# Table rows made in the stage of the keys, and attention weights put into the sums' masks

## The chip, the cores and the metric

The kernel runs on one core of one Trainium2 chip. The metric is the device time of one execution in microseconds (us). Of an engine, PE is TensorE's matmuls, PEld its weight loads, DVE is VectorE, ACT is ScalarE, POOL is GpSimd, and SP is the engine that only issues DMAs and waits.

## The reference

A stack of four graph layers over 3125 nodes with 64 features and 100000 edges, sorted by destination; each layer is followed by a residual and a layer norm. Only the first matters here, an attention layer over 8 relations:

```python
h = x @ Wr                                  # per relation r, of 8
s = h @ a_src
d = h @ a_dst
e = jax.nn.leaky_relu(s[src] + d[dst], negative_slope=0.2)
e = jnp.where(mask, e, -jnp.inf)            # mask: edges of relation r, and self loops
m = jax.ops.segment_max(e, dst, num_segments=N)
w = jnp.where(mask, jnp.exp(e - m[dst]), 0.0)
denom = jax.ops.segment_sum(w, dst, num_segments=N)
out = out + jax.ops.segment_sum((w / denom[dst])[:, None] * h[src], dst, num_segments=N) + br
```

## The kernel before, in words

Every stage is a block of five instruction streams, one per engine, written out by hand, with semaphores between them. A stage begins when all five engines have left the one before it. The order of an engine's instructions is the order of the code.

The head of the program, one stage after the other:

- `constants`: iota rows and identities.
- `edge_keys` (L142): SP loads destination, source and type of all edges. DVE makes from them a record of 7 words for each edge (`rec`, written to `meta` in DRAM) and two one-hot arrays, and PE multiplies these (98 matmuls into `hist`, L277) to count the edges of each of 196 groups of 16 nodes. The counts go to `count_row` in DRAM.
- `schedule` (L291): the counts come back to all partitions (`cnt`, L320). DVE makes from them, in some 130 small steps, the table of visits: a visit is 128 consecutive edges of one group. SP writes it (L323 to L327).
- `group_records`: it does work only if the edges are unsorted, which these are not.
- `node_tables` (L393): SP loads weights and nodes (L432). For each of 25 tiles of 128 nodes, PE makes h of all 8 relations (`h_ps`, L466) and both scores (`s_ps`, L467), ACT and DVE copy them out of PSUM into `rows` (8 relations, each 64 features, a one, and the source score: 66 words) and `score`, and SP writes the rows to `table` in DRAM. `rows` has two buffers. Then the scores go to DRAM (L445) and come back in another layout (`tab`, L449), and PE sorts them by visit with one-hot masks (`visit_hot`, L509; matmuls at L474).

Then `attention` (L702), 122 batches of 8 visits. The streams run skewed: in step n of the loop, an engine works for batches n-2 to n+4. POOL gathers the 128 table rows of each visit (`hs`, L830, six buffers, with 8 gathers in a batch). DVE makes, for all 8 visits at once, `miss` (is the edge's key not this column), and `far`, which is -2^100 at a miss and the source score at a hit (L1036). PE transposes `far` into `masked`; DVE takes its maximum (`top`, L1029); ACT turns it into a 0/1 mask in the other orientation (`hit_t`, L850), with which PE picks the maxima per edge (`picked`). From these DVE makes the exponent `lz` of each edge's weight (L1066). Beside this, for each visit PE counts neighbours (`near`, L971) into one PSUM tile that goes on from visit to visit, and ACT copies it out (`keep`, L868) before the next may be added: the matmul of visit i+1 waits for the copy of visit i, and the copy waits for the matmul. ACT also makes the 0/1 mask for the sums (`hit`, L860, two instructions of 4 visits), the weights (`weight`, L882) and the fading factors (`fade`, L891). DVE multiplies the gathered rows by the weights (`hw`, L1122), PE multiplies `hit` by `hw` (`sums`, L943), and DVE adds the result to `acc` (L1017). After each batch ACT writes eight counts to `slots` in DRAM (L873).

The other three layers follow and are not touched.

## Time and profile before

| | us |
|---|---|
| median of 3 runs (lowest, highest) | 4082.32 (4075.14, 4087.51) |
| the profiled execution | 4076.66 |
| its span | 4074.7 |
| busy in the span: PE, PEld | 2867.3, 2008.6 |
| busy in the span: DVE, ACT, POOL | 2338.2, 1459.4, 2325.4 |
| first matmul of `hist` | 44.49 |
| end of DVE's visits table | 100.07 |
| first and last row copy from `h_ps` on ACT | 126.79, 177.99 |
| last update of `acc` on DVE | 1900.2 |

The span is the time from the first to the last instruction of one execution; 1.96 us lie around it. The shares of busy time are an average over stages with different limits: the head is a chain of stages in which one engine works and the others wait, and in the attention all five work at once.

### The profile page before, as it was taken

To read this page: it belongs to the slowest core of one execution; us is meant where nothing else is said; L and a number is where in the kernel's file an instruction comes from. 1 tells how busy PE (TensorE), PEld (TensorE's weight loads), DVE (VectorE), ACT (ScalarE), POOL (GpSimd) and SP (SyncE) were. 2 spreads that over 40 slices of the span, in tenths; PEclk is the share of its full clock that TensorE was granted. 3 is DMA by queue.
4 is the path that set the end of the run, shared out by engine and by line. 5 is a ranking of instruction groups with operands and counts; after the bars stand their busy time and mean duration, and the time that the engine had idled before them with its cause. 6 is when DMAs were issued, how large, how long until landed. Compare 5 with 4: busy or idle time off the path is not lost. (4 is left out here: it accounts for less than half of the span.)

```text
span 4074.7 us, 77799 instructions
## 1 busy us (share of the span) xinstructions
PE 2867.3 (70%) x16134; PEld 2008.6 (49%) x16135; DVE 2338.2 (57%) x8613; ACT 1459.4 (36%) x3275; POOL 2325.4 (57%) x1835
## 2 busy tenths in 40 slices
PE   1627677777767677656779959887878787777752
PEld 1315455555555555444334436666666566666631
DVE  7138888888888888776342244444444444444423
ACT  0115555454455455443000004333333333333320
POOL 0046676666666666550000006888888888888880
PEclk9955555555555565556879978888888989898976
DMA  1354334333433333784614304555555555555543
GB/s 45 101 111 118 96 105 116 105 105 107 115 102 105 110 105 105 84 103 110 206 49 124 98 13 51 53 54 53 54 54 54 54 53 54 53 54 54 54 41 77
DMA packets 651838, 336.52 MB, mean 83 GB/s; under 512 B 436752, under 2 KB 612163, under 8 KB 650820
## 3 DMA queue, kind: packets, MB, share of 16 engines
q0 software_dynamic: 148736, 86.57, 22.1%
q1 hardware_dynamic: 453094, 119.03, 13.8%
q10 hardware_dynamic: 49824, 129.15, 8.3%
q14 instruction: 152, 1.25, 0.1%
q8 instruction: 32, 0.52, 0.1%
HBM read 156.42 MB, written 202.84 MB: 88 GB/s over the span
## 5 line engine op out<-in xcount | busy, mean ns | idle before, releaser
L2129 POOL DMA_INDIRECT sums<-el_rows,el_idx x816 | 1269.1, 1555 | 648.0 <-DVE el_rows L2343 399.3
L830 POOL DMA_INDIRECT at_hs<-table,at_rec_s x976 | 1048.7, 1074 | 586.7 <-issue 289.0
L971 PE MATMUL near_ps<-at_pair_hot,at_src_low_hot 128*128 128x425 f16 x976 | 498.9, 511 | 461.6 <-ACT at_count_s L868 273.3
L868 ACT CAST at_count_s<-near_ps 128x400 f16<-128x400 f32 x976 | 481.9, 494 | 874.4 <-PE near_ps L971 423.2
L2341 DVE CAST el_idx<-el_place 128x4 uint32<-128x4 f32 x204 | 35.5, 174 | 843.3 <-DMA sums<-el_rows,el_idx 795.3
L943 PEld LDWEIGHTS sums_ps<-at_hw,at_hit 128*128 128x128 f32 x1952 | 471.3, 333 | 34.1 <-issue 28.9
L943 PE MATMUL sums_ps<-at_hw,at_hit 128*128 128x66 f32 x1952 | 442.3, 408 | 8.3 <-DVE acc L1017 8.3
L971 PEld LDWEIGHTS near_ps<-at_pair_hot,at_src_low_hot 128*128 128x128 f16 x976 | 129.1, 132 | 601.1 <-ACT at_count_s L868 339.5
L1009 DVE TENSOR_SCALAR at_pair_hot<-iota_wide,at_rec_s 128x400 f16<-128x400 f16 x976 | 320.8, 331 | 1.9
L2277 ACT ACTIVATE el_h<-el_h_ps,el_valid 128x128 f32<-128x128 f32 x816 | 232.6, 368 | 237.9 <-PE el_h_ps L2191 166.6
L2145 PE MATMUL el_miss_t<-ident_b,el_miss 128*128 128x128 bf16 x816 | 83.7, 264 | 312.6 <-DVE el_miss L2315 312.6
L1017 DVE SCALAR_TENSOR_TENSOR acc<-acc,at_fade,sums_ps 128x66 f32 x976 | 268.1, 275 | 45.7 <-PE sums_ps L943 24.2
L915 PE MATMUL masked<-ident,at_far 128*128 128x128 f32 x976 | 250.4, 409 | 5.6 <-DVE at_far L1036 5.6
L2267 ACT ACTIVATE el_h<-el_h_ps,b 128x512 f32<-128x512 f32 x204 | 140.2, 687 | 316.4 <-PE el_h_ps L2180 270.6
L2202 PE MATMUL el_sum_ps<-el_h,el_join 128*128 128x128 f32 x1632 | 242.5, 296 | 7.3 <-DVE el_rows L2343 4.8
L1029 DVE TENSOR_REDUCE at_top<-masked 128x8 f32<-128x1024 f32 x122 | 149.0, 1221 | 170.6 <-issue 112.2
L2191 PE MATMUL el_h_ps<-w,el_h 128*128 128x128 f32 x1632 | 237.2, 289 | 0.0
L2177 PE MATMUL el_h_ps<-el_ea_t,w1b 64*128 64x512 f32 x408 | 233.7, 653 | 0.2 <-issue 0.2
L2325 DVE SCALAR_TENSOR_TENSOR el_join<-el_src_t,el_ends,tri 128x128 f32<-128x128 f32 x816 | 228.8, 346 | 2.1 <-PE el_src_t L2151 2.1
L2202 PEld LDWEIGHTS el_sum_ps<-el_h,el_join 128*128 128x128 f32 x1632 | 222.8, 212 | 9.5 <-issue 5.0
L2255 ACT ACTIVATE el_hit_t<-el_miss_t,ones_f 128x1024 bf16<-128x1024 bf16 x102 | 113.7, 1114 | 311.4 <-issue 199.9
L2145 PEld LDWEIGHTS el_miss_t<-ident_b,el_miss 128*128 128x128 bf16 x816 | 61.8, 118 | 330.9 <-DVE el_miss L2315 183.6
(355 smaller groups left out, 5127.1 us busy)
## 6 DMA issues: line engine op xcount, KB each, us to landing
slots<-at_count_s ACTq DMA_DIRECT2D x122, 850.0 KB
el_rec<-attr SPq DMA_DIRECT2D x816, 32.0 KB
chunk<-slots SPq DMA_DIRECT2D x240, 100.0 KB
attr<-in_edge_attr SPq DMA_DIRECT2D x19, 1248.0 KB
chunk<-slots ACTq DMA_DIRECT2D x224, 100.0 KB
at_rec_s<-meta SPq DMA_DIRECT2D x992, 3.5 KB
at_hs<-table,at_rec_s POOLq DMA_INDIRECT x976
el_pair<-meta SPq DMA_DIRECT2D x816, 1.0 KB
```

What stands on the lines that cost most here:

```text
L830: pool.indirect_dma_start(hs[:, s, u, :], None, k.table, bass.IndirectOffsetOnAxis(rec[:, s, u, 0:1].bitcast(U32), 0)).then_inc(gathered[s ...
L868: a.copy(count[:, (n.o + d) % 2, i, 0:AW], near[:, (n.o + d) % 2, 0:AW]).then_inc(count_ready, 1)
L915: t = pe.transpose(masked[:, u, :], far[:, (n.o + d) % 2, u, :], k.ident[:])
L943: m = pe.matmul(sums[:, u // 4, (u % 4) * TW:(u % 4 + 1) * TW], hit[:, s, u, :], hw[:, s, u, :], start=True, stop=True)
L971: pe.matmul(near[:, s, 0:SW], low_hot[:, s, i, :], pair_hot[:, s, i, :], start=False, stop=True, skip_group_check=(i > 0)).then_inc(near_r ...
L1009: return v.tensor_scalar(pair_hot[:, (n.o + d) % 2, u, 0:AW], k.iota_wide[:], rec[:, (n.o + d) % RING, u, 1:2], None, ALU.is_equal)
L1017: v.scalar_tensor_tensor(a, a, fade[:, (n.o + d) % 3, u:u + 1], sums[:, u // 4, (u % 4) * TW:(u % 4 + 1) * TW], ALU.mult, ALU.add).then_in ...
L2129: pool.indirect_dma_start(k.sums_flat[a], bass.IndirectOffsetOnAxis(idx[:, j, a:a + 1], 0), rows[:, j, a, :], None, compute_op=ALU.add).th ...
L2177: pe.matmul(h1_ps[:], k.w1b[:], ea_t[:, j % 2, :], start=True, stop=False)
L2191: m = pe.matmul(h2_ps[:, u * P:(u + 1) * P], h1[:, j % 2, u * P:(u + 1) * P], k.w2[:], start=False, stop=(u == 3))
L2202: m = pe.matmul(sum_ps[:, j % 2, u * P:(u + 1) * P], join[:, s, 4 * h + u, :], h2[:, j % 2, u, :], start=True, stop=True)
L2277: m = a.activation(h2[:, j % 2, u, :], h2_ps[:, u * P:(u + 1) * P], ACT.Relu, scale=valid[:, s, 4 * h + u:4 * h + u + 1])
```

## The change

`schedule` becomes a part of the stage `edge_keys`, and the making of the table rows moves there from `node_tables`. Its six loads are issued behind the loads of the edges. On PE the products of the first 12 tiles (`FIRST_TILES`) stand ahead of the matmuls of `hist`, those of the other 13 behind the matmuls of the counts. All three copies of a tile are ACT's now, which also issues its DMA to `table`, and `rows` has four buffers. The counts are written ahead of `meta`.

In the attention, ACT makes the mask of the sums with the weight already in it: exp(far * 2^-88 + lz) is the weight of the edge at a hit, where far * 2^-88 is next to nothing, and 0 at a miss, where it is -4096. Since `lz` differs from visit to visit, this takes an instruction for each visit, with `lz` as its bias: eight of 128x128 in the place of two of 128x512. `weight` and `hw` go, and PE multiplies the mask by the gathered rows `hs` themselves. The mask is made one step later than before, so `far` has three buffers, and POOL's gather into a buffer of `hs` waits for the sums that read it.

```diff
+FIRST_TILES = 12
...
+            for dst, src in ((w_t[:], k.w_t), (att[:, 0:R], k.att_src), (att[:, R:2 * R], k.att_dst), (w_cat[:], k.w_cat),
+                             (k.x_t[:], k.x_cols), (k.x_n[:], k.x_rows.rearrange("(t p) d -> p t d", p=P))):
+                sp.dma_start(dst, src).then_inc(tables_loaded, 16)
+            sp.wait_ge(count_ready, 1)
+            sp.dma_start(k.count_row.rearrange("(a b) -> a b", b=16), count[0:GW // 16, :]).then_inc(count_written, 16)
+            sp.wait_ge(count_written, 16)
+            sp.dma_start(cnt[:], k.count_row.partition_broadcast(P)).then_inc(cnt_loaded, 16)
+            sp.wait_ge(rec_ready, 1)
+            sp.dma_start(k.meta[0:EP, :].rearrange("(p j) c -> p j c", p=P), rec[:]).then_inc(rec_written, 16)
+            sp.wait_ge(pad_step, 2)
+            sp.dma_start(k.meta[EP:EP + P, :], pad_rec[:]).then_inc(rec_written, 16)
...
+        @block.scalar
+        def _(act):
+            act.wait_ge(watt_ps, 1)
+            nc.scalar.copy(w_att[:], w_ps[0:D, 0:2 * R]).then_inc(watt_ready, 1)
+            act.wait_ge(ones_ready, 1)
+            for t in range(NT):
+                act.wait_ge(h_ready, t + 1)
+                if t >= 4:
+                    act.wait_ge(row_written[t % 4], 16 * (t // 4))
+                nc.scalar.copy(rows[:, t % 4, :, 0:D], h_ps[:, t % 2, :].rearrange("p (r f) -> p r f", r=R)).then_inc(row_ready, 1)
+                nc.scalar.copy(rows[:, t % 4, :, D + 1:TW], s_ps[:, t % 2, 0:R].unsqueeze(2)).then_inc(row_ready, 1)
+                nc.scalar.copy(score[:, t], s_ps[:, t % 2, 0:2 * R].rearrange("p (w r) -> p w r", w=2)).then_inc(row_ready, 1)
+                act.wait_ge(row_ready, 3 * t + 3)
+                act.dma_start(k.table[t * P * R:(t + 1) * P * R, :].rearrange("(p r) f -> p (r f)", r=R),
+                              rows[:, t % 4].rearrange("p r f -> p (r f)")).then_inc(row_written[t % 4], 16)
+            for w in range(2):
+                act.dma_start(k.score_row[w].rearrange("(t p r) -> p t r", p=P, r=R),
+                              score[:, :, w, :]).then_inc(score_written, 16)
+            act.wait_ge(score_written, 32)
+            for i in range(4):
+                act.wait_ge(row_written[i], 16 * len(range(i, NT, 4)))
...
+            def tables(some):
+                for t in some:
+                    if t >= 2:
+                        pe.wait_ge(row_ready, 3 * t - 3)
+                    pe.matmul(h_ps[:, t % 2, :], k.x_t[:, t * P:(t + 1) * P], w_cat[:], start=True, stop=True)
+                    pe.matmul(s_ps[:, t % 2, 0:2 * R], k.x_t[:, t * P:(t + 1) * P], w_att[:], start=True,
+                              stop=True).then_inc(h_ready, 1)
+            pe.wait_ge(tables_loaded, 96)
+            for w in range(2):
+                for r in range(R):
+                    m = pe.matmul(w_ps[0:D, w * R + r:w * R + r + 1], w_t[:, r * D:(r + 1) * D],
+                                  att[:, w * R + r:w * R + r + 1], start=True, stop=True)
+            m.then_inc(watt_ps, 1)
+            pe.wait_ge(watt_ready, 1)
+            tables(range(FIRST_TILES))
...
+            pe.wait_ge(hot_ready, 2)
...
+            pe.wait_ge(count_ready, 1)
+            pe.matmul(folded[0:1, P:P + 1], k.ones_f[:, 0:1], unsorted[:], start=True, stop=True).then_inc(fold_ready, 1)
+            tables(range(FIRST_TILES, NT))
...
-            for dst, src in ((w_cat[:], k.w_cat), (w_t[:], k.w_t), (att[:, 0:R], k.att_src), (att[:, R:2 * R], k.att_dst),
-                             (k.x_t[:], k.x_cols), (k.x_n[:], k.x_rows.rearrange("(t p) d -> p t d", p=P))):
-                sp.dma_start(dst, src).then_inc(loaded, 16)
+            for w in range(2):
+                sp.dma_start(tab[:, w], k.score_row[w].rearrange("(a g n) -> g a n", a=2, n=P)).then_inc(tab_loaded, 16)
...
-            for t in range(NT):
-                sp.wait_ge(h_copied, t + 1)
-                sp.wait_ge(s_copied, t + 1)
-                sp.dma_start(k.table[t * P * R:(t + 1) * P * R, :].rearrange("(p r) f -> p (r f)", r=R),
-                             rows[:, t % 2].rearrange("p r f -> p (r f)")).then_inc(row_written[t % 2], 16)
-            for w in range(2):
-                sp.dma_start(k.score_row[w].rearrange("(t p r) -> p t r", p=P, r=R),
-                             score[:, :, w, :]).then_inc(score_written, 16)
-            sp.wait_ge(score_written, 32)
-            for w in range(2):
-                sp.dma_start(tab[:, w], k.score_row[w].rearrange("(a g n) -> g a n", a=2, n=P)).then_inc(tab_loaded, 16)
...
-        far = sb("far", [P, 2, B, P])
+        far = sb("far", [P, 3, B, P])
...
-                    pool.wait_ge(hw_ready, n(1, 1 - RING))
+                    pool.wait_ge(sums_ready, n(1, 1 - RING))
...
-            def hits(n, h):
-                s, half = n.o % 2, slice(4 * h, 4 * h + 4)
-                if h == 0:
-                    act.wait_ge(far_ready, n(1, 1))
-                    if n.after(2):
-                        act.wait_ge(sums_ready, n(1, -1))
-                a.activation(hit[:, s, half], far[:, s, half], ACT.Identity, bias=k.ones_f[:, 0:1],
-                             scale=1.0 / BIG).then_inc(hit_ready, 1)
+            def weights(n, d, i):
+                s, m = (n.o + d) % 2, (n.o + d) % 3
+                if i == 0:
+                    act.wait_ge(weight_asked, n(1, d + 1))
+                    if n.after(2 - d):
+                        act.wait_ge(sums_ready, n(1, d - 1))
+                for u in (2 * i, 2 * i + 1):
+                    w = a.activation(hit[:, s, u], far[:, m, u], ACT.Exp, bias=lz[:, s, u:u + 1], scale=2.0 ** -88)
+                if i == 3:
+                    w.then_inc(hit_ready, 1)
...
-                    act.wait_ge(weight_asked, n(1))
-                    a.activation(weight[:, (n.o + 1) % 2], lz[:, (n.o + 1) % 2], ACT.Exp).then_inc(weight_ready, 1)
+                    weights(n, -1, 0)
                 if n.has(1):
                     keep(n, 1, 2)
-                if n.has(0):
-                    hits(n, 0)
+                if n.has(-1):
+                    weights(n, -1, 1)
                 if n.has(1):
                     keep(n, 1, 3)
+                if n.has(-1):
+                    weights(n, -1, 2)
                 if n.has(0):
                     act.wait_ge(fade_asked, n(1, 1))
                     a.activation(fade[:, n.o % 3], fade_in[:, n.o % 2], ACT.Exp).then_inc(fade_ready, 1)
                 if n.has(1):
                     keep(n, 1, 4)
-                if n.has(0):
-                    hits(n, 1)
+                if n.has(-1):
+                    weights(n, -1, 3)
...
-                    pe.wait_ge(hw_ready, n(1, d + 1))
-                    pe.wait_ge(hit_ready, n(2, 2 * d + 2))
+                    pe.wait_ge(hit_ready, n(1, d + 1))
...
-                    m = pe.matmul(sums[:, u // 4, (u % 4) * TW:(u % 4 + 1) * TW], hit[:, s, u, :], hw[:, s, u, :],
+                    m = pe.matmul(sums[:, u // 4, (u % 4) * TW:(u % 4 + 1) * TW], hit[:, s, u, :], hs[:, (n.o + d) % RING, u, :],
...
-                    if n.after(1):
-                        dve.wait_ge(hit_ready, n(2))
-                    v.scalar_tensor_tensor(far[:, w], miss[:, w], -BIG, hs[:, q, :, D + 1:D + 2].to_broadcast([P, B, P]),
+                    if n.after(2):
+                        dve.wait_ge(hit_ready, n(1, -1))
+                    v.scalar_tensor_tensor(far[:, (n.o + 1) % 3], miss[:, w], -BIG, hs[:, q, :, D + 1:D + 2].to_broadcast([P, B, P]),
...
-                    if back and u == 3:
-                        dve.wait_ge(weight_ready, n(1))
-                        v.tensor_tensor(hw[:, w], hs[:, (n.o - 1) % RING],
-                                        weight[:, w].unsqueeze(2).to_broadcast([P, B, TW]), ALU.mult).then_inc(hw_ready, 1)
```

How the order on the engines changes, at three places. The first is PE's stream where the matmuls of `hist` begin. Before:

```order
L271 UNCONDITIONAL_BRANCH
L274 MATMUL hist<-zero_b 128x128
L275 UNCONDITIONAL_BRANCH
L275 ISA
L277 MATMUL hist<-low_hot,high_hot 128x128
```

Now, with the twelfth tile's two products in the first two rows:

```order
L404 MATMUL h_ps<-w_cat,x_t 128x512
L405 MATMUL s_ps<-w_att,x_t 128x16
L417 MATMUL hist<-zero_b 128x128
L418 UNCONDITIONAL_BRANCH
L418 ISA
L420 MATMUL hist<-low_hot,high_hot 128x128
```

The 16 small products of the score weights and twelve tiles stand ahead of the first matmul of `hist`, which was the first of the engine.

The second is SP's stream of DMA issues from the last load of the edges to the load of the counts. Before:

```order
L183 DMA next_i<-in_dst 128x782
L186 DMA meta<-rec 128x5474
L188 DMA meta<-pad_rec 128x7
L190 DMA count_row<-count 13x16
L142 UNCONDITIONAL_BRANCH
L318 UNCONDITIONAL_BRANCH
L320 DMA cnt<-count_row 128x208
```

Now:

```order
L214 DMA next_i<-in_dst 128x782
L218 DMA w_t<-in_w_t 64x512
L218 DMA att<-in_att_src 64x8
L218 DMA att<-in_att_dst 64x8
L218 DMA w_cat<-in_w_cat 64x512
L218 DMA x_t<-in_x_cols 64x3200
L218 DMA x_n<-in_x_rows 128x25x64
L220 DMA count_row<-count 13x16
L222 DMA cnt<-count_row 128x208
L224 DMA meta<-rec 128x5474
L226 DMA meta<-pad_rec 128x7
```

The loads of the tables come in behind those of the edges, and the counts go out and come back ahead of the records.

The third is ACT's stream in one step of the attention, from the copies of visits 0 and 1 (L868) to that of visit 5. Before:

```order
L868 CAST at_count_s<-near_ps 128x400 x2
L882 ACTIVATE at_weight<-at_lz 128x8
L868 CAST at_count_s<-near_ps 128x400
L860 ACTIVATE at_hit<-at_far,ones_f 128x512
L868 CAST at_count_s<-near_ps 128x400
L891 ACTIVATE at_fade<-at_fade_in 128x8
L868 CAST at_count_s<-near_ps 128x400
L860 ACTIVATE at_hit<-at_far,ones_f 128x512
L868 CAST at_count_s<-near_ps 128x400
```

Now:

```order
L848 CAST at_count_s<-near_ps 128x400 x2
L839 ACTIVATE at_hit<-at_far,at_lz 128x128 x2
L848 CAST at_count_s<-near_ps 128x400
L839 ACTIVATE at_hit<-at_far,at_lz 128x128 x2
L848 CAST at_count_s<-near_ps 128x400
L839 ACTIVATE at_hit<-at_far,at_lz 128x128 x2
L872 ACTIVATE at_fade<-at_fade_in 128x8
L848 CAST at_count_s<-near_ps 128x400
L839 ACTIVATE at_hit<-at_far,at_lz 128x128 x2
L848 CAST at_count_s<-near_ps 128x400
```

Four pairs of small instructions stand in four gaps between the copies, where a small one, two wide ones and the fading factor stood.

## Rows read from the trace of the kernel before

**Rows 1.** Timeline of the head: start, length (us), engine, line, what [idle before]

```profile
8.70 0.43 SPq L183 DMA_DIRECT2D next_i<-in_dst  x1
14.64 0.57 DVE L213 TENSOR_SCALAR tmp_i<-dst_i 128x782 int32<-128x782 int32 x1 [14.53 <-DMA next_i<-in_dst]
44.49 0.29 PE L274 MATMUL hist<-zero_b 128*128 128x128 bf16 x1 [44.49 <-DVE low_hot L226]
...
63.36 0.28 PE L280 MATMUL hist<-zero_b 128*128 128x128 bf16 x1
63.79 0.29 DVE L257 COPY pair<-hist 128x128 f32<-128x128 f32 x1 [2.58 <-PE hist L280]
...
66.32 0.37 SPq L190 DMA_DIRECT2D count_row<-count  x1
...
107.61 0.56 SPq L432 DMA_DIRECT2D w_cat<-in_w_cat  x1
...
111.40 6.34 SPq L434 DMA_DIRECT2D group_b<-visit_f  x1
...
120.61 3.57 PE L458 MATMUL v_ps<-att,w_t 64*64 64x1 f32 x32 [54.08 <-DMA x_n<-in_x_rows]
...
124.44 2.07 PE L466 MATMUL h_ps<-w_cat,x_t 64*128 64x512 f32 x2 [0.26 <-DVE w_att L493]
...
178.16 0.25 DVE L502 CAST over_row<-start_row 1x128 f32<-1x128 int32 x1
...
178.97 2.45 SPq L445 DMA_DIRECT2D score_row<-score  x2
...
179.55 1.54 DVE L509 TENSOR_SCALAR visit_hot<-group_b,hundred 100x1024 f32<-100x1024 f32 x2
...
185.62 0.75 SPq L449 DMA_DIRECT2D tab<-score_row  x2
...
188.31 10.09 PE L474 MATMUL v_ps<-visit_hot,tab 100*128 100x512 f32 x16 [10.36 <-DMA tab<-score_row]
```

**Rows 2.** Groups by line, whole span: busy us, mean ns | idle before, releasers

```profile
L466 PE MATMUL h_ps<-w_cat,x_t 64*128 64x512 f32 x50 | 51.3, 1127 | 0.3 <-DVE w_att L493 0.3
...
L1788 PE MATMUL msg_prod<-agg_t,msg_w_msg 128*64 128x512 f32 (+1 forms) x42 | 20.6, 572 | 0.0
...
L484 ACT COPY rows<-h_ps 128x512 f32<-128x512 f32 x25 | 14.7, 587 | 55.0 <-PE s_ps L467 55.0
```

**Rows 3.** One stretch of the attention: PE, PEld, DVE, ACT, POOL busy, PEclk

```profile
400.00:800.00 400.00, 285.20 (x1297) 212.45 (x1296) 350.06 (x1265) 202.32 (x463) 269.45 (x247) 0.56 0.39 109
```

**Rows 4.** Groups by line in the same stretch, 400 to 800 us

```profile
L830 POOL DMA_INDIRECT at_hs<-table,at_rec_s x247 | 271.3, 1098 | 130.9 <-issue 68.6 <-PE near_ps L971 40.3 <-remote 21.9
L971 PE MATMUL near_ps<-at_pair_hot,at_src_low_hot 128*128 128x425 f16 x247 | 127.3, 515 | 92.5 <-ACT at_count_s L868 62.0 <-issue 28.8 <-DVE at_pair_hot L1009 1.0
L868 ACT CAST at_count_s<-near_ps 128x400 f16<-128x400 f32 x247 | 122.0, 494 | 194.1 <-PE near_ps L971 91.7 <-issue 49.3 <-remote 49.2
...
L860 ACT ACTIVATE at_hit<-at_far,ones_f 128x512 f32<-128x512 f32 x62 | 44.9, 724 | 0.0
...
L1029 DVE TENSOR_REDUCE at_top<-masked 128x8 f32<-128x1024 f32 x31 | 37.9, 1222 | 38.1 <-issue 21.3 <-ACT at_hit_t L850 16.4
...
L1122 DVE TENSOR_TENSOR at_hw<-at_hs,at_weight 128x528 f32<-128x528 f32 x30 | 20.9, 697 | 0.0
...
L882 ACT ACTIVATE at_weight<-at_lz 128x8 f32<-128x8 f32 x31 | 6.6, 211 | 3.0 <-DVE at_lz L1066 2.3 <-issue 0.7
```

**Rows 5.** Timeline of ACT in one step of the attention

```profile
1006.09 0.49 ACT L868 CAST at_count_s<-near_ps 128x400 f16<-128x400 f32 x1 [0.61 <-PE near_ps L971]
...
1006.48 0.72 ACT L860 ACTIVATE at_hit<-at_far,ones_f 128x512 f32<-128x512 f32 x1
...
1007.10 0.48 ACT L868 CAST at_count_s<-near_ps 128x400 f16<-128x400 f32 x1
```

**Rows 6.** Timeline of ACT in the last layer: four small ACTIVATEs in a row

```profile
3014.40 1.14 ACT L2277 ACTIVATE el_h<-el_h_ps,el_valid 128x128 f32<-128x128 f32 x4 [0.72 <-PE el_h_ps L2191]
```

More of the change, by code:

```diff
@@ L175, in edge_keys @@
         pad_step = sem("pad_step")
+        cnt = sb("cnt", [P, GW])
+        cnt3 = sb("cnt3", [P, GW // 8])
+        up_i = sb("up_i", [P, GW], I32)
+        visits = sb("visits", [P, GW])
+        ends = sb("ends", [P, GW])
+        short = sb("short", [P, GW])
+        zeros = sb("zeros", [P, GW])
+        ones = sb("ones", [P, GW])
+        scrap = sb("scrap", [P, GW])
+        group = sb("group", [P, 2, B])
+        off = sb("off", [P, 2, B])
+        table_i = sb("table_i", [P, 4, B], I32)
+        start_i = sb("start_own", [P, 4], I32)
+        begin = sb("begin", [P, B])
+        since = sb("since", [P, 1])
+        part = sb("part", [P, 1])
+        over = sb("over", [P, 4])
+        cnt_loaded, step_sem, ready, written = sem("sched_loaded"), sem("sched_step"), sem("table_ready"), sem("table_written")
+        w_cat = sb("w_cat", [D, R * D])
+        w_t = sb("w_t", [D, R * D])
+        att = sb("att", [D, 2 * R])
+        w_att = sb("w_att", [D, 2 * R])
+        rows = sb("rows", [P, 4, R, TW])
+        score = sb("score", [P, NT, 2, R])
+        h_ps = c.enter_context(nc.psum_tensor("h_ps", [P, 2, CW], F32))
+        s_ps = c.enter_context(nc.psum_tensor("s_ps", [P, 2, CW], F32))
+        w_ps = c.enter_context(nc.psum_tensor("w_ps", [P, CW], F32))
+        tables_loaded, watt_ps, watt_ready = sem("tables_loaded"), sem("watt_ps"), sem("watt_ready")
+        h_ready, row_ready, ones_ready, score_written = sem("h_ready"), sem("row_ready"), sem("ones_ready"), sem("score_written")
+        row_written = [sem(f"row_written{i}") for i in range(4)]
         block = c.enter_context(nc.Block())
@@ L211, in _ @@
             v = nc.vector
+            v.memset(rows[:, :, :, D:D + 1], 1.0).then_inc(ones_ready, 1)
             dve.wait_ge(loaded, 64)
@@ L391, in _ @@
             v.tensor_copy(scrap[:, 0:1], zeros[:, 0:1]).then_inc(ready, 1)
+        @block.scalar
[17 more added lines that the diff above has]
+            act.wait_ge(score_written, 32)
+            for i in range(4):
+                act.wait_ge(row_written[i], 16 * len(range(i, NT, 4)))
@@ L476, in _ @@
             m.then_inc(by_visit_ready, 1)
-        @block.scalar
-        def _(act):
-            for t in range(NT):
-                act.wait_ge(h_ready, t + 1)
-                if t >= 2:
-                    act.wait_ge(row_written[t % 2], 16 * (t // 2))
-                nc.scalar.copy(rows[:, t % 2, :, 0:D], h_ps[:, t % 2, :].rearrange("p (r f) -> p r f", r=R)).then_inc(h_copied, 1)
         @block.vector
@@ L739, in attention @@
         lz = sb("lz", [P, 2, B])
-        weight = sb("weight", [P, 2, B])
-        hw = sb("hw", [P, 2, B, TW])
         masked = ps("masked", [P, B, P])
```

125 lines of the change are left out of this document (24 added, 101 removed).

## Prediction

> **What bounds the kernel now.** I read the timeline of the head first, since that is where most of the moved work stands. The reader is to see a relay: DVE begins at 14.64 us, PE has nothing to do until 44.49, DVE waits 2.58 us for the end of `hist` at 63.64 (63.36 + 0.28), then comes the visits table, which is DVE's alone, and only at 107.61 does the loading for the tables begin. PE makes 25 tiles from 124.44 to about 178.16, nothing else in the program can begin, and then the scores travel to DRAM and back, until PE starts on them at 188.31 [rows 1]. So 188.31 is the end of one chain, and PE, which makes the tiles, was idle for most of the 107 us before.
>
> Then the groups of one stretch of the attention, 400 to 800 us, with 31 batches (31 of `top`), so 12.9 us a batch. DVE is busy for 350 of 400 us [rows 3], and one would call it the bound. The waits say otherwise: DVE itself waits 38.1 us before `top`, while PE's `near` waits 62.0 us for ACT's copies and 1.0 us for DVE; ACT's copies wait 91.7 us for `near`, 49.3 without a releaser and 49.2 for "remote"; and ACT waits 2.3 us for DVE before `weight` [rows 4]. The loop goes at the pace of the hand-over between `near` and its copy, 8 times a batch. DVE mostly catches up behind it.
>
> **The head, step by step.** The six loads of the tables took 13.0 us from the first issue to PE's start (107.61 to 120.61). Now they are issued behind the last edge load, from 9.13 on (8.70 + 0.43) [rows 1]. They are in at 22.1 if the edge loads don't hold them up, and at 27.6 if they only begin when those have landed (14.64 + 13.0); I take 25, near the middle. The first tile comes 3.83 us later (120.61 to 124.44), at 28.8. A tile takes 2.15 us (53.7 us for 25), so 12 take 25.8 and end at 54.6 [rows 1]. ACT's added copies and the DMA issue don't lengthen it: the wide copy is 587 ns [rows 2], the two narrow ones at most 211 each as the narrow `weight` [rows 4], an issue 0.3 to 0.6 [rows 1]; that is 1.6 us of 2.15.
>
> Here stands the cost: `hist` could begin at 44.49 and now begins at 54.6. Its length, 19.15 us (44.49 to 63.64), is unchanged, so it ends at 73.8, 10.1 us later, and DVE, which waits for it already, passes all of that on. By the bounds of the loads it is 7.2 to 12.7. The way from there through the visits table to the next stage keeps its length: one barrier less, and the loads of the counts only have the table rows' writes beside them, both of which I cost at nothing. The next stage begins at 107.6 + 10.1 = 117.7.
>
> The other 13 tiles take 27.9 us from 76.9 (the counts, 66.32 + 10.1, and a small matmul) to 104.8. They lie beside DVE's visits table. The scores' way out took 6.65 us (178.97 to 185.62), so they are in DRAM at about 112, and 5 to 6 us of cover are left. If the table rows were later than that, each further us would count in full.
>
> In the next stage only the loads for the visits are left. Before, they stood behind the big ones (issue of `group_b` 6.34 us) but had landed long before the tiles ended, so no row has their price. Low: issued by about 120.7 and landed 2.7 us later like `tab` (185.62 to 188.31), at 123.4. High: 13.0 us like the six loads, 130.7. I take the middle, 127. DVE then needs 2.93 us until both masks are there (178.16 to 179.55 + 1.54), and PE starts at 129.9 instead of 188.31 [rows 1]. `tab` was asked for first and is there. **The head gives 58.4 us**; with both bounds at either end, 52 to 65.
>
> **The attention.** DVE loses `hw`, 697 ns a batch [rows 4], 122 times 0.697 = 85 us. That is one end, and nothing is the other, as DVE already waits 1.2 us a batch. The gain can only come where somebody waits for DVE: 1.0 + 2.3 us in 31 batches, or 13 us in 122, and of a long wait only 0.7 goes. I take 8 us, near the low end, since that row is the nearest.
>
> ACT loses two wide masks, at 0.62 us from start to start (1006.48 to 1007.10) [rows 5], and `weight` (0.21), together 1.45 a batch. It gets eight small ones. No row has an exponential of 128x128 with a bias from memory; the nearest is the four of 128x128 in a row in 1.14 us, at most 0.285 each [rows 6]. So 2.28 a batch, 0.83 more. ACT idles 0.79 us before each copy (194.1 over 247) [rows 4], 6.3 a batch. A pair is 0.57 and takes less than the wide mask's 0.62 in the same gap; only the gap that also holds the fading factor gets longer, 0.57 + 0.21 against the 0.62 that fits in another gap. Bounds: 12 us less (0.05 twice a batch), if ACT is the later one in both gaps, and 0.83 times 122 = 101 us more, if all of it fell on the hand-over. I take 0, by the idle time.
>
> The new wait: POOL's gathers of a batch stand behind the sums of six batches before, no longer behind `hw`. Behind that wait are only POOL's own gathers, and DVE's `far` waits for those. POOL uses 10.96 us of 12.9 a batch (271.3 + 68.6 in 31) [rows 4] and works three batches ahead, so a start that is some us later is made up. Cost 0. If the lead didn't cover it, at most the slack of 2 us a batch would turn into the same wait on DVE, which has 1.2 of its own. The third buffer of `far` takes away a wait that no row shows.
>
> **Sum.** 4076.66 - 58.4 - 8 = 4010.3 for the profiled execution. The median is 5.66 above the profiled one (4082.32 - 4076.66), so 4015.9: **4016 us**.
>
> **A rule of the skill that speaks against it.** The row gives 0.724 us for a wide mask with a bias from memory [rows 4], and at most 0.285 from start to start for a small one [rows 6]. The Trainium skill (ScalarE: Activation LUTs, What ACT_TABLE_LOAD costs) says that an ACTIVATE with such a bias takes about 280 ns plus 0.833 ns an element, less some 93 ns of overlap; its 707 ns for 512 elements agrees with the row. By it each of the eight costs 294 ns, 2.35 a batch, and were all of that on the hand-over, it would be 110 us and 4126 in total.
>
> **Rivals.**
> *ACT becomes the pace (slower).* The place is the four gaps between the copies of visits 1 to 5. For it: `near` already waits 62.0 us for these copies in 31 batches, more than for anything else [rows 4], and three ACTIVATEs become eight. The price is up to 0.83 a batch, 101 us: 4016 + 101 = 4117. It decides from 66.4 / 122 = 0.54 us a batch on; below, the head's gain outweighs it. Against it: the 0.79 us of idle time before each copy. A half of the price gives 4066.
> *DVE was the bound after all.* For it: 350 of 400 us busy [rows 3]. Then the whole 85 us come: 4016 - 77 = 3939. Against it: its 38.1 us before `top`, and nobody's waits for it.
> *PE runs the tiles at the higher clock.* A 512-column matmul of a tile takes 1127 ns, one of a later stage 572 [rows 2], the two levels 1.2 and 2.4 GHz; the tiles had 53.7 us without a pause and stayed at the lower one. If the twelve ran at the higher one, a tile would take 1.09 us and all of them 13.1, they would end at 41.9, before 44.49, and the 10.1 us would not be lost: 4006. The Trainium skill (TensorE: Matmul & The Clock Gate, What's actually happening) says that sustained work brings the higher clock. By that rule 4006 would be the likelier time; for these tiles the trace does not agree.
> *The visits' loads or `hist` come later than I have it,* both at their worst ends: 4022.
>
> **How the numbers follow.** The forecast, with the late loads within it, has 0.70, its own range 3998 to 4036; the clock 0.06; DVE as the bound, in whole or half, 0.09; ACT as the pace 0.15, of which a third beyond 0.54 us a batch. The hand-over is also hit by "remote" stalls of 49.2 us in 31 batches, 1.6 each [rows 4]; a fifth more or fewer of them is 39 us either way, and that I put into the range. It goes from 3966 (half of the DVE case) to 4056 (some four tenths of the ACT case). A measurement of this kernel tells about 0.3% (12 us) from no change. Faster 0.92, within 0.04, slower 0.04.
>
> **What would show it.** In the trace after: first tile at about 28.8, `hist` from about 54.6 to 73.8, first DMA of the next stage at 117.7, the visits' matmuls at 129.9, first update of `acc` some 58 us earlier. In the attention: DVE's wait before `top` grows by about 0.6 us a batch, the period stays within 0.1 of 12.9, small exponentials take 0.25 to 0.29 from start to start. I am wrong if PE waits for `hit`, if POOL's gathers make DVE wait before `far`, or if the waits of `near` for ACT grow by more than 0.2 us a batch.

## The result and the profile after

The changed kernel takes 4155.78 us (median of 4 runs, 4155.01 to 4156.47) beside 4078.73 for the kernel before: a ratio of 1.0186, 95% interval 1.0167 to 1.0205. It is slower by 77 us where I forecast 63 to 66 us less. The profiled spans are 4154.7 and 4074.7 us.

Where the 80 us between the spans lie, by the start of the weights of the first and the last `near`: the first comes at 203.0 instead of 266.5 (63.6 us earlier), from the first to the last it takes 1757.1 instead of 1610.9 us (146.2 more), and what follows takes 2194.7 instead of 2197.2 (2.5 less). The head did what was forecast, the attention lost more than twice that.

The head, from the timeline of the changed kernel (start, duration, engine, line and operation, and in brackets the idle time before it and what ended it):

```profile
23.65 3.57 PE L411 MATMUL w_ps<-att,w_t 64*64 64x1 f32 x32 [23.65 <-DMA x_n<-in_x_rows]
27.48 2.07 PE L404 MATMUL h_ps<-w_cat,x_t 64*128 64x512 f32 x2 [0.26 <-ACT w_att L378]
53.19 0.29 PE L417 MATMUL hist<-zero_b 128*128 128x128 bf16 x1
69.64 0.28 PE L423 MATMUL hist<-zero_b 128*128 128x128 bf16 x1
70.06 0.29 DVE L301 COPY pair<-hist 128x128 f32<-128x128 f32 x1 [7.81 <-PE hist L423]
113.21 0.74 SPq L458 DMA_DIRECT2D tab<-score_row  x2
121.01 0.26 DVE L483 CAST over_row<-start_row 1x128 f32<-1x128 int32 x1 [7.23 <-DMA slots<-none]
124.10 1.19 PE L473 MATMUL v_ps<-visit_hot,tab 100*128 100x512 f32 x1 [23.41 <-DVE visit_hot L490]
```

They stand beside [rows 1]. The loads are in at 23.65 (I took 25), the first tile begins at 27.48 (28.8), `hist` at 53.19 (54.6) and it ends at 69.92 (73.8): its matmuls took 16.7 us and not 19.15. The next stage starts at 113.21 (117.7) and the visits' matmuls at 124.10 (129.9), 64.2 us before the 188.31 of [rows 1].

The attention from 400 to 800 us, first the busy time in that window (PE, PEld, DVE, ACT, POOL, then the granted clock of PE, the DMA share and GB/s), beside [rows 3]:

```profile
400.00:800.00 400.00, 256.48 (x1182) 193.74 (x1180) 300.76 (x1121) 212.20 (x565) 238.56 (x226) 0.58 0.36 98
```

Then its groups, beside [rows 4] (busy us, mean ns, idle us before them and what ended it):

```profile
L808 POOL DMA_INDIRECT at_hs<-table,at_rec_s x226 | 239.7, 1061 | 161.7 <-PE near_ps L951 78.1 <-issue 54.4 <-remote 22.6
L951 PE MATMUL near_ps<-at_pair_hot,at_src_low_hot 128*128 128x425 f16 x226 | 115.7, 512 | 123.8 <-ACT at_count_s L848 92.3 <-issue 31.1
L848 ACT CAST at_count_s<-near_ps 128x400 f16<-128x400 f32 x225 | 111.1, 494 | 187.8 <-remote 97.3 <-issue 47.7 <-PE near_ps L951 37.2
L839 ACT ACTIVATE at_hit<-at_far,at_lz 128x128 f32<-128x128 f32 x226 | 78.3, 397 | 0.0
L1009 DVE TENSOR_REDUCE at_top<-masked 128x8 f32<-128x1024 f32 x28 | 34.3, 1225 | 82.5 <-ACT at_hit_t L828 61.1 <-issue 21.5
```

Only 28 batches fit where 31 did: 14.3 us a batch instead of 12.9. Every engine is less busy, except ACT; DVE waits 2.9 us a batch before `top` (1.2 before). No engine has become the bound. Nor are the exponentials what stretches the hand-over: they start every 0.304 us (median), a little above my 0.285, and the median time from one copy of the counts to the next is as before in each of the eight places (1.96, 1.96, 1.21, 1.21, 1.12, 1.12, 1.12, 1.93). What has doubled is the "remote" part of the wait of ACT's copies, from 49.2 to 97.3 us, and POOL's wait for `near`, from 40.3 to 78.1 us. "Remote" is what the profile writes where a wait ends by the update of a counter (a semaphore) and no instruction ended close before that update. This program has one core, so another core is not meant. All 80 copies whose wait ends so between 400 and 1600 us wait for the one counter that the matmul of `near` raises.

One of these waits in the timeline of the changed kernel, ACT, PE and POOL:

```profile
1004.35 0.49 ACT L848 CAST at_count_s<-near_ps 128x400 f16<-128x400 f32 x1
1004.90 0.35 PE L951 MATMUL near_ps<-at_pair_hot,at_src_low_hot 128*128 128x425 f16 x1 [0.50 <-ACT at_count_s L848]
1005.41 0.95 POOL L808 DMA_INDIRECT at_hs<-table,at_rec_s  x1 [0.31 <-issue]
1006.67 0.95 POOL L808 DMA_INDIRECT at_hs<-table,at_rec_s  x1 [0.30 <-issue]
1007.92 0.95 POOL L808 DMA_INDIRECT at_hs<-table,at_rec_s  x1 [0.30 <-issue]
1010.18 0.49 ACT L848 CAST at_count_s<-near_ps 128x400 f16<-128x400 f32 x1 [4.64 <-remote]
1010.57 0.69 ACT L828 ACTIVATE at_hit_t<-masked,ones_f 128x512 bf16<-128x512 f32 x1
1010.94 0.95 POOL L808 DMA_INDIRECT at_hs<-table,at_rec_s  x1 [2.07 <-remote]
1011.37 1.23 DVE L1009 TENSOR_REDUCE at_top<-masked 128x8 f32<-128x1024 f32 x1 [6.48 <-ACT at_hit_t L828]
```

The matmul ends at about 1005.25, its copy begins at 1010.18. The trace has the counter's update at 1010.16. In between POOL gathers without a pause, until its own wait, for the same counter, stops it at 1008.87; 1.3 us later the update comes, and both go on. DVE's 6.48 us are a consequence: it waits for ACT's second mask of this batch, which stands behind the late copy and ends at 1011.27. What is late is PE's signal. (The ends of matmuls are modelled in the profile, so whether the matmul itself or only its signal took longer can't be told.) The signal the other way is not late: between 400 and 1600 us no `near` behind the first of a batch starts more than 0.7 us after the copy that it waits for and PE's own work. I call a late start of a copy a stall, and count one where a copy starts over 1.3 us after the weights of its `near` (its time from 0.5 us after them, between 400 and 1600 us of the trace). The kernel before has 110 with 205 of 1200 us, the changed one 103 with 294: 1.9 us each, and now 2.9. Over a batch that is 2.2 and 3.5 us, and 1.3 times 122 is about the loss. Of the 205 us, 126 end "remote" (54 stalls), of the 294 it is 254 (80 stalls). Before, such a stall had mostly one gather in it (37 of 54), now mostly two or three (69 of 80). It ends when POOL has gone idle in 50 of the 54 and in 62 of the 80, 1.1 and 1.2 us (median) after the end of POOL's last gather; in the other 18 a gather is still running.

And POOL's gathers come otherwise. Before, the first gather of a batch started 2.3 us (median) after the weights of the first count that it waits for, plus 0.5, and the eight were 1.58 us apart. Now it starts 6.1 us after, and they are 1.43 apart: POOL now waits for the sums, which PE multiplies only behind the second count of a batch, and by then the counts that gate the next gathers are done. So it issues without pauses.

### The profile page after: what moved, and what is told of

It reads as the page before. It is cut to its first block and busy times, and to the rows that moved or that the text cites. A ratio compares the mean times of both kernels' runs of the same rounds, so it can differ in the third digit from the quotient of the medians.

```text
span 4154.7 us, 78113 instructions
## 1 busy us (share of the span) xinstructions
PE 2853.5 (69%) x16134; PEld 2011.4 (48%) x16135; DVE 2257.9 (54%) x8440; ACT 1584.3 (38%) x3936; POOL 2309.6 (56%) x1835
## 3 DMA queue, kind: packets, MB, share of 16 engines
q14 instruction: 152, 1.25, 0.1%
## 5 line engine op out<-in xcount | busy, mean ns | idle before, releaser
L808 POOL DMA_INDIRECT at_hs<-table,at_rec_s x976 | 1031.8, 1057 | 754.7 <-PE near_ps L951 409.2
L951 PEld LDWEIGHTS near_ps<-at_pair_hot,at_src_low_hot 128*128 128x128 f16 x976 | 129.9, 133 | 747.1 <-ACT at_count_s L848 448.6
L923 PEld LDWEIGHTS sums_ps<-at_hs,at_hit 128*128 128x128 f32 x1952 | 472.9, 333 | 34.7 <-issue 30.1
L923 PE MATMUL sums_ps<-at_hs,at_hit 128*128 128x66 f32 x1952 | 442.2, 408 | 7.9 <-DVE acc L997 7.9
L839 ACT ACTIVATE at_hit<-at_far,at_lz 128x128 f32<-128x128 f32 x976 | 337.7, 396 | 18.3 <-DVE at_lz L1046 18.3
```

The lines of the kernel that those rows point to most:

```text
L808: pool.indirect_dma_start(hs[:, s, u, :], None, k.table, bass.IndirectOffsetOnAxis(rec[:, s, u, 0:1].bitcast(U32), 0)).then_inc(gathered[s ...
L839: w = a.activation(hit[:, s, u], far[:, m, u], ACT.Exp, bias=lz[:, s, u:u + 1], scale=2.0 ** -88)
L923: m = pe.matmul(sums[:, u // 4, (u % 4) * TW:(u % 4 + 1) * TW], hit[:, s, u, :], hs[:, (n.o + d) % RING, u, :], start=True, stop=True)
L951: pe.matmul(near[:, s, 0:SW], low_hot[:, s, i, :], pair_hot[:, s, i, :], start=False, stop=True, skip_group_check=(i > 0)).then_inc(near_r ...
```

## The experiments

Three ideas were at hand. The first is called W in the expectations: POOL's new wait for the sums comes last, the gathers run without pauses, and the stalls last as long as they run. Its rival, X: ScalarE's eight exponentials. Later came C (the stalls are SyncE's record loads meeting the gathers) against G (the gathers alone).

The chips were of two kinds. On those of the first comparison and of e1 to e4, r1 to r4 and s1 to s4 the kernel before took 4079 to 4097 us; on those of e5 to e8 and of t1 and t2 it took 3991. I call the second kind quiet, for not one copy waits for a late signal there. A ratio is to the kernel before on the same chip, with its 95% interval. "Attention" is from the first to the last `near` in us. "Late" is the part of the stalls that ends "remote". "A batch" is the mean time of the batches 14 to 109 in us. The changed kernel as it stands had no run on a quiet chip.

| label | kernel | ratio | attention | stalls, of 1200 us | late | a batch |
|---|---|---|---|---|---|---|
| | before | 1 | 1610.9 | 205 | 126 | 12.95 |
| | after | 1.0186 (1.0167 to 1.0205) | 1757.1 | 294 | 254 | 14.34 |
| r1_after | after | 1.0180 (1.0160 to 1.0200) | 1761.3 | 295 | 247 | 14.39 |
| s1_after | after | 1.0192 (1.0155 to 1.0229) | 1769.9 | 299 | 247 | 14.43 |
| e1_head | head alone | 0.9850 (0.9829 to 0.9871) | 1648.1 | 233 | 195 | 13.29 |
| s4_head | head alone | 0.9858 (0.9827 to 0.9889) | 1616.0 | 227 | 175 | 13.02 |
| e2_sumswait | before, new wait | 1.0227 (1.0203 to 1.0250) | 1737.6 | 302 | 191 | 14.17 |
| e3_lead2 | after, LEAD 2 | 0.9879 (0.9857 to 0.9900) | 1647.2 | 235 | 169 | 13.30 |
| r2_lead2 | after, LEAD 2 | 0.9856 (0.9834 to 0.9878) | 1630.0 | 227 | 177 | 13.13 |
| e4_ring8 | after, 8 buffers | 0.9912 (0.9891 to 0.9934) | 1650.0 | 247 | 187 | 13.38 |
| r4_lead21 | after, 21 visits | 0.9834 (0.9814 to 0.9855) | 1613.8 | 207 | 152 | 12.99 |
| r3_pace | LEAD 2, paced loads | 0.9895 (0.9875 to 0.9915) | 1636.4 | 240 | 179 | 13.18 |
| s2_oneload | after, one load | 0.9967 (0.9951 to 0.9982) | 1681.8 | 290 | 249 | 13.97 |
| s3_half | after, half the gathers | 0.9318 (0.9291 to 0.9344) | 1408.9 | 20 | 0 | 11.59 |
| e5_oneload (quiet) | after, one load | 0.9495 (0.9480 to 0.9511) | 1401.7 | 30 | 0 | 11.55 |
| e6_pace (quiet) | LEAD 2, paced loads | 0.9672 (0.9656 to 0.9688) | 1467.1 | 68 | 0 | 11.57 |
| e7_border (quiet) | LEAD 2, held loads | 0.9666 (0.9645 to 0.9688) | 1466.6 | 72 | 0 | 11.61 |
| e8_lead21 (quiet) | after, 21 visits | 0.9653 (0.9637 to 0.9669) | 1457.8 | 70 | 0 | 11.55 |
| t1_new21 (quiet) | after, 21 visits | 0.9666 (0.9653 to 0.9679) | 1463.2 | 79 | 0 | 11.58 |
| t2_old21 (quiet) | head alone, 21 visits | 0.9857 (0.9842 to 0.9872) | 1534.1 | 81 | 0 | 12.31 |

On the quiet chips no copy's wait ends "remote". What the count still finds there comes once in six batches, at the turn of the loop (17 stalls in t1, 15 of them 1.2 to 2.3 us long), and late in the attention, where the copy waits for the DMA that writes the counts. The copies from 400 to 800 us in t1, beside the line of the changed kernel above:

```profile
L848 ACT CAST at_count_s<-near_ps 128x400 f16<-128x400 f32 x276 | 136.3, 494 | 128.5 <-PE near_ps L951 123.1
```

**The head alone** (e1_head, s4_head): the changed kernel with `attention` as it was before.

> The merged head with the attention as it was before (no exponentials into the masks, the 128x528 multiply back on VectorE, GpSimd gated by that multiply). Theory W (GpSimd's new wait for the sums) and theory X (ScalarE's eight exponentials) agree: the head's 64 us that the trace shows (PE at its last table work 188.31 before, 124.10 after) stay, the attention's loss goes; 4078.7 - 64 = 4015 us, within 8. If the loss were a side effect of the head (buffers or schedule rows placed elsewhere), it would stay near 4155.

> The merged head with the attention of before, beside the changed kernel on one chip: 0.967 of the changed kernel (0.985 to 1.0186 of before).

Both chips give it: the head is worth 1.4 to 1.5%, 58 to 62 us by the ratios, 59 and 52 by the medians. s4's attention is that of the kernel before (1616.0 beside 1610.9); e1's is 1648.1, on the chip on which the kernel before is 18 us slower and has no trace.

**The new wait alone** (e2_sumswait), in the kernel before:

```diff
-                    pool.wait_ge(hw_ready, n(1, 1 - RING))
+                    pool.wait_ge(sums_ready, n(1, 1 - RING))
```

> The kernel before with one edit: GpSimd's gathers wait for the sums of the batch six back and not for the multiply ahead of them. Theory W: the gathers now start two visits late, run 6 or 8 in a row instead of 1 to 4, and the hand-over from TensorE to ScalarE stands still while they run; nearly all of the attention's loss of about 141 us appears, 4190 to 4220 us. Theory X: nothing changes, 4079 within 6 us.

4194.53 us beside 4097.06. One wait, with everything else as before, costs 2.3% or 97 us. That is two thirds of the attention's 146, where I had expected nearly all. Its stalls are 302 of 1200 us, and its first gather comes 6.3 us after, the others 1.40 apart. The link to the gathers is looser here: only 35 of its 66 stalls that end "remote" end with POOL idle. Its groups from 400 to 800 us:

```profile
L830 POOL DMA_INDIRECT at_hs<-table,at_rec_s x230 | 253.1, 1100 | 149.6 <-PE near_ps L971 81.6 <-issue 57.9 <-remote 10.1
L868 ACT CAST at_count_s<-near_ps 128x400 f16<-128x400 f32 x231 | 114.2, 495 | 213.7 <-PE near_ps L971 100.2 <-remote 75.3 <-issue 35.1
```

POOL waits 81.6 us for `near` (40.3 before [rows 4]), as in the changed kernel. X gives no change here and falls as the cause of the whole.

**The wait made harmless in three ways** (e3_lead2, r2_lead2; e4_ring8; e8_lead21, r4_lead21), each in the changed kernel with its exponentials:

```diff
-LEAD = 3
+LEAD = 2                # e3, r2
-RING = 6
+RING = 8                # e4
-                        pool.wait_ge(near_ready, n(B, u + 1 - LEAD * B))
+                        pool.wait_ge(near_ready, n(B, u + 1 - 21))    # e8, r4, t1
```

With eight buffers the loop no longer meets the three of `far` and `fade` in the same turn, so that e4 mixes the values of batches; its time alone is read.

> The changed kernel with the gathers two batches ahead of the counts and not three (LEAD 2): the sums that GpSimd waits for are then done a batch earlier, so that wait is never the last. Theory W: the gathers are again paced by the counts one by one, the stalls shrink to those of before, 4000 to 4030 us. Theory X: ScalarE is as full as in the changed kernel, 4155 within 10 us. A third possibility: gathers 13 us later come too late for `far`; then VectorE waits for the gathers and the time is above 4155.

> The changed kernel with eight buffers for the records and the gathered rows and not six: GpSimd waits for the sums of the batch eight back, done long before, while the gathers keep their lead of three batches. Theory W: as with the shorter lead, 4000 to 4030 us. Theory X: 4155 within 10 us.

> The changed kernel with one number: a gather waits for the count 21 visits back and not 24, so that the first gather of a batch starts when the sums that it also waits for are done, and the others follow the counts one by one instead of running free. Theory W: runs and stalls as short as before, 4020 to 4060 us. If any late start of the gathers costs time, or if the wait for the sums still comes last: above 4100.

> The changed kernel again, on the chip of the three runs beside it, since the kernel before differs by 100 us between the chips so far (4097 and 3991). Theories W and C: on any chip it is slower than the same attention with paced gathers; if this chip's hand-overs stand still less, it loses less than the 1.0186 of the first comparison.

> LEAD 2 in the changed kernel, beside the changed kernel on one chip. Theory W: 0.97 of the changed kernel (0.9879 to 1.0186 of before). If the recovery had come from the chip: 1.00.

> The gathers 21 visits behind the counts, record loads as in the changed kernel. Theory W: as LEAD 2 alone within 0.3%, whichever chip.

All three take nearly all of the loss away: 0.983 to 0.991 on the chips with stalls, against 1.018 of the changed kernel. On the chip of e1, e3 and e4 something is left: 4048.52 and 4062.05 us beside 4038.30 of the head alone, both above the 4000 to 4030 of the expectation. r1, r2 and r4 ran on one chip: 4152.95, 4022.39 and 4011.37 us. The eight exponentials are in each of them. r4's groups from 400 to 800 us:

```profile
L808 POOL DMA_INDIRECT at_hs<-table,at_rec_s x245 | 261.4, 1067 | 138.7 <-issue 76.2 <-remote 43.1 <-PE near_ps L951 19.4
L951 PE MATMUL near_ps<-at_pair_hot,at_src_low_hot 128*128 128x425 f16 x246 | 123.5, 502 | 98.1 <-ACT at_count_s L848 67.2 <-issue 30.1
L848 ACT CAST at_count_s<-near_ps 128x400 f16<-128x400 f32 x246 | 121.4, 493 | 170.0 <-remote 67.9 <-issue 54.3 <-PE near_ps L951 42.9
L839 ACT ACTIVATE at_hit<-at_far,at_lz 128x128 f32<-128x128 f32 x244 | 84.6, 397 | 0.9 <-DVE at_lz L1046 0.4 <-issue 0.4
```

The same exponentials, and 31 batches again. Its gathers are 1.63 us apart and start 8.1 us after the count that gated the old ones, 2 later than in the changed kernel. So a late start is not what costs; a start behind counts that are already done is, on such a chip. e8's 3851 us fall outside its expectation, which did not foresee the quiet chip.

**SyncE's loads moved** (e6_pace, r3_pace, e7_border), with LEAD 2: one by one behind the counts, or all eight behind the last count.

```diff
+                    if n.after(RING - d):
+                        sp.wait_ge(near_ready, n(B, (d - RING) * B + u + 1))   # e6, r3, for each u
+                    sp.wait_ge(near_ready, n(B, (d - RING) * B + B))           # e7, once
```

> The changed kernel with LEAD 2, and each of SyncE's record loads issued only once the count of the like-numbered visit of the batch six back is done: loads one by one instead of eight in a row. Theory C with the length of the collision as its price: single loads of 0.33 us leave no room for a long stall, 3900 to 4000 us. Theory G: 4048 as with LEAD 2 alone, within 10 us. A third possibility: each single load costs a short stall of its own, eight a batch, and the time is above 4060.

> The changed kernel with LEAD 2, and the eight record loads held until the last count of a batch is done, where GpSimd has the least to issue (it waits for the next batch's first count about 2.7 us later). Theory C: fewer gathers meet the loads, 4000 to 4040 us. Theory G: 4048 within 10 us.

> LEAD 2 and the record loads one by one behind the counts. Theory C: 0.97 to 0.99 of LEAD 2 alone on this chip, with SyncE's slow issues gone. Theory G: the same time as LEAD 2 alone.

On the quiet chip neither differs from e8, whose loads stand where they stood, but there is no late signal to take away there, so e6 and e7 test nothing. r3 does: beside r2 the paced loads are no faster (4033.65 and 4022.39). C has nothing here.

**One load for eight, and half the gathers** (e5_oneload, s2_oneload; s3_half), in the changed kernel. The one load leaves out which records belong to a visit, the half leaves out every second visit's rows:

```diff
-                for u in range(B):
-                    sp.dma_start(rec[:, s, u, :], k.meta[bass.ds(offs[u], P), :])...
+                sp.dma_start(rec[:, s]..., k.meta[bass.ds(n(768, 768 * d), B * P), :]...)   # e5, s2
-                for u in range(B):
+                for u in range(0, B, 2):                                                   # s3, POOL
```

> The changed kernel with one transfer of a batch's records on SyncE in place of eight, from evenly spaced rows of the list (it leaves out which records belong to a visit, so its output isn't the reference's; bytes and gathers stay). Theory C, the stalls are a collision: hand-overs between engines stand still where SyncE issues its eight loads while GpSimd issues gathers back to back; with one load in place of eight the stalls (294 of 1200 us in the changed kernel) shrink below 100 and the batch goes from 14.3 towards the 11.3 us that an undisturbed batch takes: 3800 to 3950 us. Theory G, the gathers alone do it: 4155 within 20 us.

> One record load of a batch in place of eight, beside the changed kernel on one chip (leaves out which records belong to a visit). Theory C: stalls below 100 of 1200 us and 0.92 to 0.95 of the changed kernel. Theory G: stalls stay near 290, the same time within 0.5%.

> The changed kernel with four gathers a batch and not eight; the other four visits take rows of zeros (that half of the gathered rows is left out). SyncE's eight loads stay. Theory C and theory G agree that the stalls shrink, since each needs GpSimd's runs: below 100 of 1200 us, 0.92 to 0.95 of the changed kernel. If the stalls stay near 290, the gathers have no part in them and SyncE's loads alone make them.

> The changed kernel, as the yardstick for the runs beside it on this chip: 1.018 of the kernel before where that takes about 4080 us; on a chip where that takes about 3990, fewer stalls and a smaller loss.

e5 seemed to confirm C, but it had a quiet chip. s2, s3 and s1 ran on one of the other kind. Groups from 400 to 800 us, of s2:

```profile
L808 POOL DMA_INDIRECT at_hs<-table,at_rec_s x227 | 242.6, 1069 | 158.2 <-PE near_ps L951 81.6 <-issue 56.0 <-remote 18.0
L848 ACT CAST at_count_s<-near_ps 128x400 f16<-128x400 f32 x229 | 112.9, 493 | 185.4 <-remote 97.4 <-PE near_ps L951 52.7 <-issue 30.1
```

and of s3:

```profile
L808 POOL DMA_INDIRECT at_hs<-table,at_rec_s x139 | 150.8, 1085 | 247.4 <-PE near_ps L951 222.5 <-issue 25.0
L848 ACT CAST at_count_s<-near_ps 128x400 f16<-128x400 f32 x276 | 135.9, 492 | 130.5 <-PE near_ps L951 124.0 <-issue 0.9
L1009 DVE TENSOR_REDUCE at_top<-masked 128x8 f32<-128x1024 f32 x35 | 42.8, 1222 | 24.8 <-issue 20.1 <-ACT at_hit_t L828 4.3
```

One load leaves the "remote" wait of the copies at 97.4 us and the stalls at 290 of 1200: C falls. Its time is 0.977 of s1's, which neither C nor G had. Partly that is the head's (its first `near` comes at 184.9 instead of 202.3), partly 88 us of attention (1681.8 beside 1769.9). Of these, 39 lie in the last 12 batches: they take 190 to 204 us in every run with its true records and all gathers, whatever the chip, and 159 in s2, 140 in e5. Since these two read other records, that says nothing of the loads. Of the other 49 us I have no account. With four gathers a batch the "remote" wait is gone, stalls are 20 of 1200, and 35 batches fit: 11.59 us a batch, the pace of the quiet chips (11.58 in t1). On these chips the late signals need POOL's gathers, and they do not need SyncE's loads. s3 halves the number of the gathers, their rows and the length of their runs together, so which of the three counts it does not tell; that the spacing matters at the same number is e2 and r4.

e5 shows one thing more. It has the changed kernel's wait for the sums, its gathers start 6.1 us late and are 1.43 apart, and on its quiet chip a batch takes 11.55 us, as in e8, whose wait is harmless. There the runs of gathers cost nothing; it has one load in place of eight, so it is a sign of what the changed kernel would do there and not a measurement of it.

**The price of the exponentials** (t1_new21, t2_old21): the same head, the same spacing of the gathers, the attention's new and old way of weighing.

> Weights by exponentials into the masks, gathers 21 visits behind the counts: 0.983 of the kernel before where that takes about 4080 us (as measured before on such a chip), 0.965 where it takes 3990. If the exponentials bring what the prediction gave them, 8 us below the kernel beside it; if ScalarE pays for them, above it.

> The merged head, weights by the multiply on VectorE as before, gathers 21 visits behind the counts. If shorter spacing is itself good, below the head with the old spacing (0.985 to 0.986 of before); else the same. Prediction's step: 8 us above the kernel beside it; exponentials free and worthless: within 4 us of it.

A quiet chip, and neither expectation holds: 3861.45 beside 3932.78, 71 us for the new way. Both are of one chip, and the attention takes 1463.2 and 1534.1 us, all of the difference. Groups from 400 to 800 us, of t1:

```profile
L951 PE MATMUL near_ps<-at_pair_hot,at_src_low_hot 128*128 128x425 f16 x276 | 137.2, 497 | 67.0 <-ACT at_count_s L848 66.2
L839 ACT ACTIVATE at_hit<-at_far,at_lz 128x128 f32<-128x128 f32 x274 | 95.0, 396 | 14.5 <-DVE at_lz L1046 14.2
```

and of t2:

```profile
L952 PE MATMUL near_ps<-at_pair_hot,at_src_low_hot 128*128 128x425 f16 x260 | 129.9, 500 | 67.9 <-ACT at_count_s L849 61.6 <-DVE at_pair_hot L990 5.2
L896 PE MATMUL masked<-ident,at_far 128*128 128x128 f32 x264 | 67.2, 407 | 12.7 <-DVE at_far L1017 12.7
L863 ACT ACTIVATE at_weight<-at_lz 128x8 f32<-128x8 f32 x32 | 6.7, 208 | 40.2 <-DVE at_lz L1047 32.7 <-issue 7.5
```

In t2 three things wait for DVE: `near` 5.2 us, the transposes 12.7 and `weight` 32.7. Without the stalls DVE is the bound in t2, and the multiply of 0.695 us a batch that goes gives 0.73 in the batches 14 to 109 (12.31 to 11.58) and nothing in the last 12 (201 and 199 us). Where the stalls are frequent, the gain doesn't show: e3 is no faster than e1 on their chip (4048.52 and 4038.30), and r4's ratio is within the interval of s4's. That DVE makes up for the multiply in the stalls fits this and is not shown; no two runs on such a chip differ in the way of weighing alone.

## Why the prediction was wrong

- **The head gives 58.4 us.** Right: 64.2 in the trace, 58 to 62 in the ratio of the head alone. Too careful were the length of `hist`, which I called unchanged (16.7 for 19.15), and the loads for the visits (a stage that begins at 113.2 has its masks at 124.1, in 10.9 us and not 12.2).
- **The new wait costs nothing: this step failed.** The words were that "a start that is some us later is made up". It is made up, and DVE never waits for POOL before `far` (0.0 us in 28 batches). But it is made up by running without pauses, and on these chips PE's signal that a count is done then comes up to 5 us late, mostly only after POOL has run dry. I had read the "remote" stalls of [rows 4] and put a fifth of them, 39 us, into the range; I took them for a thing of the chip on which the change has no hold. By the same rows they went from 1.6 us a batch (49.2 in 31) to 3.5 (97.3 in 28), and all stalls from 2.2 to 3.5. None of the rivals had this; the only slower one was ACT's. The prediction asked whether somebody would wait for POOL, and not what POOL does when it has nothing to wait for. e2 shows the wait alone at 2.3%; the changed kernel takes 3.4% more than the head alone (s1 and s4). The remaining 1% also goes, or nearly, when the wait is made harmless (e3, e4, r4), so it needs the wait; why the exponentials beside it make it larger was not settled.
- **ACT costs 0, ACT as the pace (0.15).** Right to take 0, and the rival did not come: r4 has the exponentials and is at 0.983. The start-to-start time of 0.304 us lies above my upper bound of 0.285. An estimate from the figures of the Trainium skill (ScalarE: Activation LUTs, What ACT_TABLE_LOAD costs), 280 ns plus 0.833 ns an element less 93 ns, is 0.294 us; this trace stands 0.010 above that.
- **`hw` gives 8 us.** Mis-sized, and by the chip: 71 us on a quiet one, where the rival that DVE was the bound (3939) is the true one, and about 10 on the others (s4 and r4, on two chips, with intervals that allow anything from 0 to 25). The reading of who waits for whom in [rows 4] was right for the trace it came from.
- **PE at the higher clock.** Not here: 12 tiles took 25.7 us (27.48 to 53.19), 2.14 each, as forecast with the lower one. The profile prints a granted clock of 1.00 for both heads, but its records of the clock begin only at 194.3 us in the kernel before and at 130.2 in the changed one. At just these times the visits' matmuls of 512 columns go from 1061 to about 593 ns. So until then PE ran at the lower level of 1.2 GHz, through 53.7 us of tiles before and 25.7 now.
- **The low end of the range, 3966,** is called half of the DVE case; half of its 77 us gives 3977.
- **The signs that I named.** I was to be wrong "if the waits of `near` for ACT grow by more than 0.2 us a batch": they went from 2.0 to 3.3 (92.3 / 28). And "the period stays within 0.1 of 12.9": it is 14.3. The other two signs, PE waiting for `hit` and DVE waiting before `far`, did not come.

## What to carry to other kernels

Before a wait of the engine that issues gathers is moved, ask which of its other waits it makes idle: waits that open one by one space the gathers, and one that opens late turns them into a run. Long waits that end with no releaser on the core are a term of the sum, not noise; look at what runs while they last. A version with 21 visits in place of 24 keeps the head's gain on both kinds of chip and takes the multiply's on the quiet ones: 0.9834 (0.9814 to 0.9855) of the kernel before where signals come late, 0.9666 (0.9653 to 0.9679) where they don't. And two kernels are compared on one chip: the ratio of the same pair can differ between chips when another engine is the bound there.

## What the runs showed of the hardware that was not expected

- While POOL issues indirect DMAs back to back (0.95 us each, 1.25 apart), PE's signal of a finished matmul can reach ACT and POOL up to 5 us late: 254 of 1200 us in the changed kernel, 126 in the kernel before, none with half the gathers (s3). ACT's signals to PE are not late in the same stretch (0.7 us at most from the copy to the next `near`). Whether it is the issuing or the transfers that it sets off, no run separates.
- SyncE is held up beside it: in the changed kernel 225 of its 1694 register instructions between 400 and 1600 us take 0.6 us or more, mostly 0.70, in s3 14 of 2013, in t1 none. With one load in place of eight the stalls stay, so that is a companion and not the cause.
- Only some chips do it. On the quiet ones t1 has up to 19 gathers with starts less than 1.5 us apart (9 in the changed kernel) and no late signal at all. What differs between the chips no run shows. The traces of the others also lack records: of 976 updates of the counter of `near`, 684 are there in the changed kernel, 866 in s3 and 975 in t1. So a part of the recording itself in the stalls is not ruled out.
- The kernel before, unchanged, took 3991 us on two chips, and 4079 to 4097 on three others and in the first comparison.
